# A sandwich of latent attention and a ternary feed-forward layer: another order for the chain of tiles 2 and 3 before the first feed-forward stage, and the signs of four weight pieces on GpSimd

## What is computed

```python
def reference(hidden_states, Wq, bq, Wk, bk, Wv, bv, Wo, bo, latent_keys, W_up, W_gate, W_down):
    def attn(h):                                   # h [2, 2048, 512], 16 heads of 32
        Q, V = h @ Wq.T + bq, h @ Wv.T + bv
        logits = einsum('bhtd,lhd->bhtl', Q, latent) / sqrt(32)      # 64 latents per head
        top, idx = top_k(logits, 4)
        weighted = softmax(top) @ latent[idx]
        return (weighted + V) @ Wo.T + bo
    def ternary(w):
        scale = mean(abs(w)) + 1e-8
        return clip(round(w / scale), -1, 1) * scale
    def ffn(h):                                    # 512 -> 2048 -> 512
        return (silu(h @ ternary(W_up).T) * (h @ ternary(W_gate).T)) @ ternary(W_down).T
    x = x + layernorm(attn(layernorm(x)))
    return x + layernorm(ffn(layernorm(x)))
```

## Time and profile before

| | |
|---|---|
| three executions | 1032.02, 1033.41 (median), 1034.98 us |
| the profiled execution | 1034.87 us, its span 1033.0 us |
| mean granted TensorE clock | 0.982 |
| PE busy | 968.6 us (94%) |
| DVE, ACT, POOL busy | 729.7, 514.2, 535.9 us |

### The profile page before, as it was taken

How to read it: one execution, slowest core, us unless ns; L and a number is a source line. 1 busy time by engine, 2 the same in 40 slices (tenths; PEclk the granted TensorE clock), 3 DMA queues, 4 the chain that set the end, 5 groups by cost and what they waited for, 6 DMA issues and landing times.

```text
span 1033.0 us, 17908 instructions
## 1 busy us (share of the span) xinstructions
PE 968.6 (94%) x5738; PEld 470.2 (46%) x5738; DVE 729.7 (71%) x2665; ACT 514.2 (50%) x801; POOL 535.9 (52%) x452
## 2 busy tenths in 40 slices
PE   3738899999999999999999999999999999999997
PEld 2413444445444554445444454445444454445443
DVE  7998699366993689755993768836895669845433
ACT  5887886445535455245544455345553454423430
POOL 3566256645565446564565446654465546642330
PEclk9869899999999999999999999999999999999999
DMA  9963503442134402234114321253022411212001
GB/s 289 401 110 62 154 1 82 115 90 82 22 42 102 107 16 41 61 81 102 21 21 102 71 72 21 41 118 96 10 41 61 94 40 21 42 41 62 1 1 41
DMA packets 149330, 76.91 MB, mean 74 GB/s; under 512 B 135824, under 2 KB 135824, under 8 KB 148112
## 3 DMA queue, kind: packets, MB, share of 16 engines
q1 hardware_dynamic: 149264, 76.18, 29.7%
HBM read 34.21 MB, written 8.39 MB: 41 GB/s over the span
## 4 chain that ended last, share of the span: by engine, by line
PE 52%; DVE 21%; issue 8%; POOL 8%; ACT 7%; DMA 3%; SPq 0%; DVEq 0%; ACTq 0%; POOLq 0%
PE ug L709 33%; PE ug L728 9%; PE ring L559 6%; DVE Lr L1581 2%; PE ring L687 2%; PE ring L605 2%; POOL halves L1297 2%; DMA X1T<-halves 2%; DVE halves L1535 2%; DVE v L1555 1%; DVE row L1672 1%; DVE x L1692 1%; DVE stx L1695 1%; DVE sty L1675 1%; DVE ugt L1540 1%
## 5 line engine op out<-in xcount | busy, mean ns | idle before, releaser
L709 PE MATMUL ug<-X1T,TU 128*128 128x512 f16 (+1 forms) x1152 | 246.7, 357 | 11.0 <-DMA X1T<-halves 6.7
L1274 POOL TENSOR_TENSOR hT<-ugt,hT 128x512 f16<-128x512 f32 x128 | 167.1, 1305 | 165.6 <-ACT hT L1026 165.6
L709 PE MATMUL ug<-X1T,TG 128*128 128x512 f16 (+1 forms) x1152 | 245.7, 356 | 0.0
L728 PE MATMUL ug<-TD,hT 128*128 128x512 f16 x960 | 210.9, 379 | 0.9 <-ACT TD L905 0.9
L1013 ACT ACTIVATE ugt<-ug,cu 128x512 f32<-128x512 f32 x128 | 88.0, 687 | 207.5 <-PE ug L709 206.6
L709 PEld LDWEIGHTS ug<-X1T,TU 128*128 128x128 f16 x1152 | 110.6, 98 | 122.1 <-issue 9.9
L709 PEld LDWEIGHTS ug<-X1T,TG 128*128 128x128 f16 x1152 | 113.2, 98 | 109.1
L1540 DVE SCALAR_TENSOR_TENSOR ugt<-ugt,ug 128x512 f32<-128x512 f32 x128 | 87.3, 682 | 103.3 <-ACT ugt L1013 102.0
L728 PEld LDWEIGHTS ug<-TD,hT 128*128 128x128 f16 x960 | 93.2, 98 | 115.8 <-issue 3.0
L1581 DVE MATCH_REPLACE8 Lr<-v,Lb 128x68 f32<-128x68 f32 x512 | 102.3, 212 | 0.0
L1545 DVE SCALAR_TENSOR_TENSOR ugt<-ugt,ug 128x512 f32<-128x512 f32 x128 | 87.9, 687 | 4.4
(11 more groups left out here) (217 smaller groups left out, 1498.7 us busy)
## 6 DMA issues: line engine op xcount, KB each, us to landing
out_dram<-Lr SPq DMA_DIRECT2D x32, 256.0 KB, 3.2
x_in<-in_x SPq DMA_DIRECT2D x7, 1024.0 KB, 5.3
x<-in_x SPq DMA_DIRECT2D x28, 256.0 KB, 3.3
PT<-in_Wd SPq DMA_DIRECT2D x8, 512.0 KB, 7.2
hT<-in_Wu SPq DMA_DIRECT2D x4, 512.0 KB, 9.2
hT<-in_Wg SPq DMA_DIRECT2D x4, 512.0 KB, 15.2
x_in<-in_Wd SPq DMA_DIRECT2D x4, 512.0 KB, 4.8
x_in<-in_x SPq DMA_DIRECT2D x4, 256.0 KB, 4.1
```

Source lines behind the costliest of these rows:

```text
L709: last = pe.matmul(ug[:, 2 * (e % 2) + s, cols], w[:, k, e * P:(e + 1) * P], X1T[:, b, k, cols], start=(k == 0 and b == 0), stop=(k == KD ...
L728: last = pe.matmul(down_bank(kind, t), hT[:, a, e, t * P:(t + 1) * P], td[:, e, :], start=(first and e == of[0] and a == 0), stop=(final a ...
L1274: pool.tensor_tensor(hT[:, 1, e, :], ugt[:, 2 + e % 2, :], hT[:, 0, e, :], ALU.subtract).then_inc(h_lo, 1)
```

## The change

It has two parts.

In the first body, DVE does `y_a(2)` before `y_b(1)`, `y_a(3)` before the low half of tile 0, and both `y_b` and all `y_c` of tiles 2 and 3 ahead of every rounding but that of piece 8. ACT does `t2_rows` of tile 2 right behind `q(0)`, that of tile 3 right behind `q(1)`, and the signs of 1 and 9 after both. The rounding of piece 8 goes from POOL to DVE, that of piece 0 stands further ahead on POOL.

In the second body's loop, the signs of pieces 6, 14, 7 and 15 go from ACT to POOL, as two `TENSOR_SCALAR` passes over 1024 elements each (`sign_of`): one in place in float32 (add, max with -1), one that writes the float16 matrix (min with 1). They stand behind `hidden_lo` of `e` = 2, 3, 5 and 6. DVE's roundings of 11, 6 and 14 stand earlier, and ACT has the signs of 10, 5 and 3 one step earlier.

```diff
+        SIGN_POOL = (6, 14, 7, 15)
+        def after_pool(n):
+            return len(ROUND_POOL) + 2 * SIGN_POOL.index(n) + 2
...
+                        if e // 2 in SIGN_POOL:
+                            pe.wait_ge(pool_step, after_pool(NPIECE + e // 2))
...
+                    if kind == "second" and e in (8, 12):
+                        act.wait_ge(pool_step, after_pool(e // 4 + 4))
...
-                SIGN_AT = {0: (2,), 1: (10,), 2: (5, 13), 3: (3, 11), 4: (6,), 5: (14,), 6: (7, 15), 8: (22,), ...
+                SIGN_AT = {0: (2, 10), 1: (5,), 2: (13, 3), 3: (11,), 8: (22,), ...
...
+                def sign_of(n):
+
+                    src = stages[n // NPIECE][n % NPIECE]
+                    pool.wait_ge(rounded, rounded_before(n))
+                    pool.tensor_scalar(src, src, -MAGIC, -1.0, ALU.add, ALU.max).then_inc(pool_step, 1)
+                    pool.wait_ge(pool_step, after_pool(n) - 1)
+                    pool.tensor_scalar(matrix(n), source(n), 1.0, None, ALU.min).then_inc(pool_step, 1)
...
+                    if late and e in (2, 3, 5, 6):
+                        sign_of(SIGN_POOL[(2, 3, 5, 6).index(e)])
...
-                    AFTER = {0: [(round_to, 3)], 1: [(round_to, 11)], 2: [(round_to, 6), (maxes, 0, 0), (maxes, 0, 1)],
-                             3: [(round_to, 14), (slots, 0), (replace, 0, 0)], 4: ...
+                    AFTER = {0: [(round_to, 3), (round_to, 11)], 1: [(round_to, 6), (round_to, 14)], 2: [(maxes, 0, 0), (maxes, 0, 1)],
+                             3: [(slots, 0), (replace, 0, 0)], 4: ...
```

More of the change, by code:

```diff
@@ L273, in build @@
         ASUM_ACT = (0, 1, 16, 17, 18, 19) + tuple(range(4, 14)) + tuple(range(20, 24))
-        TERN_ORDER = (0, 8, 1, 9, 4, 12, 2, 10, 5, 13, 3, 11, 6, 14, 7, 15, 22, 23, 16, 17, 20, 21, 18, 19)
+        TERN_ORDER = (0, 8, 1, 9, 4, 12, 2, 10, 5, 13, 3, 11, 22, 23, 16, 17, 20, 21, 18, 19)
         ROUND_ACT = (18, 19)
-        ROUND_POOL = (0, 8)
+        ROUND_POOL = (0,)
+        SIGN_POOL = (6, 14, 7, 15)
+        ROUND_ORDER = (8, 1, 9, 4, 12, 2, 10, 5, 13, 3, 11, 6, 14, 7, 15, 22, 23, 16, 17, 20, 21)
+        def after_pool(n):
+            return len(ROUND_POOL) + 2 * SIGN_POOL.index(n) + 2
         def rounded_before(n):
-            return sum(q not in ROUND_POOL for q in TERN_ORDER[:TERN_ORDER.index(n) + 1])
+            return ROUND_ORDER.index(n) + 1
         def after_tern(*pieces):
@@ L1101, in body @@
                     q(0)
-                    sign(1)
                     t2_rows(-1, 2)
-                    sign(9)
                     q(1)
                     t2_rows(-1, 3)
+                    sign(1)
+                    sign(9)
+                    q(2)
                     sign(4)
-                    q(2)
                     sign(12)
@@ L1269, in round_to @@
                     pool.wait_ge(tern_scale, w + 1)
-                    pool.tensor_scalar(src, src, iw[:, w:w + 1], MAGIC, ALU.mult, ALU.add).then_inc(pool_rounded, 1)
+                    pool.tensor_scalar(src, src, iw[:, w:w + 1], MAGIC, ALU.mult, ALU.add).then_inc(pool_step, 1)
+                def sign_of(n):
[4 more added lines that the diff above has]
+                    pool.tensor_scalar(matrix(n), source(n), 1.0, None, ALU.min).then_inc(pool_step, 1)
                 def hidden_lo(e):
                     wait(pool, h_hi, j, NE, e + 1)
+                    if kind == "second" and e in (8, 12):
+                        pool.wait_ge(pool_step, after_pool(e // 4 + 12))
                     pool.tensor_tensor(hT[:, 1, e, :], ugt[:, 2 + e % 2, :], hT[:, 0, e, :], ALU.subtract).then_inc(h_lo, 1)
@@ L1776, in body @@
                     y_b(0)
+                    y_a(2)
+                    y_c(0, 0)
+                    tern_total(1)
                     y_b(1)
-                    y_c(0, 0)
+                    y_a(3)
+                    t2_lo(0, 0)
                     y_c(0, 1)
[L1780 to L1783, removed]
                     tern_scale_of(1)
-                    round_to(1)
+                    round_to(8)
                     y_b(2)
                     t2_lo(0, 1)
+                    y_c(0, 2)
+                    y_b(3)
+                    t2_lo(0, 2)
+                    y_c(0, 3)
+                    round_to(1)
+                    t2_lo(0, 3)
                     round_to(9)
-                    y_b(3)
-                    y_c(0, 2)
                     round_to(4)
-                    y_c(0, 3)
-                    t2_lo(0, 2)
                     round_to(12)
-                    t2_lo(0, 3)
                     round_to(2)
```

16 lines of the change are left out of this document (8 added, 8 removed).

## The result

The changed kernel took **1042.72 us** (median of five executions, 1041.86 to 1044.28), against 1033.41 before (five executions, 1032.02 to 1036.05): ratio 1.0089, 95% interval 1.0074 to 1.0105. It is slower by 9.3 us. The forecast was 1032.4, with a range of 1029.2 to 1035.0, so the time lies far outside, on the slow side. The profiled execution took 1042.75 us, its span is 1040.6.

The account below looks back on a forecast made before the run. PE, busy 94% of the span, was taken to bound the kernel, with ACT and then DVE setting the loop's pace. The sum 6.4 - 0.9 - 4.6 + 0.1 = 1.0 us gave 1032.4 us, range 1029.2 to 1035.0.

Parts of the forecast that it names:

- the opening: First body: PE's 4.1 us wait for transposed tiles 2 and 3 goes, its clock stays up, `upgate(2)` starts 6.4 us earlier.
- 3.34 for the transfer: Opening: time from DVE's last operation on tile 3 at 102.4 until PE can go on, at 105.75.
- a pass of two float32 operations over 1024 elements took POOL 1.12 us: Loop, GpSimd's signs: the price of each sign's first pass, taken from a row of the trace.
- 1.3 for the second: Loop, GpSimd's signs: assumed price in us of the float16 pass, making four signs 10.0 us.
- The bound above, 2.14: Loop, GpSimd's signs: upper bound in us for the float16 pass, from a float16 operation on two inputs.
- own signs of being wrong: Wrong if `ffn_scales` stays short, POOL has pauses before 140, or a float16 pass costs far from 1.3 us.
- In itself that delays nobody: Loop: POOL's lump of signs, without pause until about 143.7, delays nobody, as pieces 6 and 14 are needed only by `upgate(12)`.
- The lock: Loop, `hidden(5)` to `hidden(8)`: DVE's operations wait for GpSimd's, 4.8 us less 0.3 idle; `hidden(8)` 0.9 us ahead instead of 5.5.
- rounding of 15 as before: Loop, behind `hidden(5)`: the first of DVE's seven operations open to blocking keeps its time.
- PE's new wait: Loop, near 143: PE waits some 4.5 us for `hidden(8)`, its clock falls, and `upgate(10)` starts at 147.0.
- Rival B: Loop: slower, since the second pass costs 2.14 and DVE's turns lengthen; 1036 to 1037 us, chance 0.11.
- Rival A: Loop: the gain is kept, as POOL isn't full at `ffn_scales` or DVE wins turns; 1029 to 1030 us, chance 0.27.

Follow-up runs that it names:

- e1: The changed kernel with the signs of 6, 14, 7 and 15 back on ACT, new opening and tables kept: 1028.73 us, 0.9955 of the kernel before.
- e5: The change's new opening alone, with the loop tables of the kernel before and all signs on ACT: 1029.12 us, 0.9958 of before.
- e3: The changed kernel with GpSimd's first pass a multiply-add and its second a multiply alone, pieces not clipped: 1035.23 us, 1.0013 of before.
- e8: The changed kernel with both GpSimd passes as multiply-adds, pieces not cut to signs: 1032.61 us, 0.9992 of before.
- e7: The changed kernel with GpSimd's eight passes one behind each low half of tiles 2 to 9: 1042.11 us, 1.0080 of before.
- e13: The changed kernel with the four signs made by no engine, PE reading columns of tiles 4 to 7 again: 1031.15 us, 0.9970 of before.
- e14: As e13, with one wait more that holds GpSimd's shift until the rounding of piece 15 is done: 1028.91 us, 0.9953 of before.
- e11: The changed kernel with one multiply-add a piece on GpSimd, straight to the matrix, not cut to signs: 1032.21 us, 0.9982 of before.

## Why the prediction was wrong

**What bounds the kernel, and the opening: right, with one duration too small.** Sign of 8 ended at 94.8 (forecast 95.1), tile 3's low half at 102.53 (102.4), `tanh(4)` came at 124.37 (123.9). PE's wait fell to 0.89 us and its clock stayed up at 107 to 108. The term "3.34 for the transfer" was too small: from DVE's last low half to PE it takes 4.87 us (102.53 to 107.40), of which the last transposes are 4.58 in the chain, and why they took longer in the new order isn't shown. So PE goes on at 107.40, not 105.75, and `upgate(2)` is 4.85 us earlier, not 6.4. By their ratios the whole gains 4.6 us in e1 and 4.3 in e5.

**The step that failed: "a pass of two float32 operations over 1024 elements took POOL 1.12 us", and 1.3 for the second.** The row was a multiply-add; the change's pass is an add and a max. It takes 3.64, and the second 2.77: four signs are 26 us, not 10.0. The price was taken from a row of the same instruction and shape with other operations in it. The bound above, 2.14, was too low as well, and for the first pass no bound was given, since the row was taken for its own. e3 and e8 show each half of this: with the first pass at 1.04 the time is 1035.2, with both at 1.04 it is 1032.6. So of the 14.0 us that the signs cost, 10.1 are the price of the passes. Two of the prediction's own signs of being wrong came with it: a float16 pass far from 1.3 us, and short `ffn_scales`.

The Trainium skill (GPSIMD Engine Reference, 3.1 Elementwise), by which up to two operations cost 1.03 cycles an element (an estimate of 0.88 us for 1024), agrees with the 1.04 to 1.06 of multiply-add, add-multiply and copy. For the other forms the measured 2.78 and 3.63 or more decide against it.

**"In itself that delays nobody" falls with the price.** It was reasoned from when the pieces are needed. The queue behind the passes was counted for the lock only, while the low halves in it release DVE's next buffer. At 10 us it would have held: in e8 DVE waits for no low half. At 26 us it cost 8.9 us of waits on DVE, and PE's two long waits with the low clock behind them. e7 shows that the low halves are not the only ones in the queue: spread out, the same passes delay the shift, at the same cost.

**The lock (DVE's operations that wait out one of GpSimd's): a right sum with a wrong cause.** The prediction put 4.6 us on DVE between `hidden(5)` and `hidden(8)` and left `hidden(8)` 0.9 us ahead. With its own prices (e8) it was 3.93, and `hidden(8)` started at 145.44 (forecast 145.55). But "rounding of 15 as before" was wrong: 2.40 us in place of 0.94. And e13 shows 2.87 (14.57 against 11.70) of the 3.93 with no pass at all, e14 that one meeting with the shift starts it. The prediction named the passes; they add only the rest. In the changed kernel itself the slow passes held DVE less than forecast: `ffn_scales` at 147.34 took 0.15 us with the second pass of piece 7 under way since 145.83. The holds that it did have are the slots' difference (1.16 us at 141.07 for 0.16), `select(0)` (2.07 for 1.21) and the rounding of 22 (1.56 at 145.85 for 0.75): 2.7 us where 4.8 were forecast.

**PE's new wait, and luck in e8's time.** With the prediction's prices (e8) PE waits 1.67 us for DVE's scale (`sw`) at 141.31 and 1.28 for `hidden(8)`, not 4.5 in one piece, and the granted clock is 1.00 in each microsecond from 140 to 149, so nothing is lost to a low clock. `upgate(10)` starts at 146.98, as forecast (147.0), but by errors that cancel: `upgate(2)` was 4.43 us ahead in place of 6.4, and `hidden(5)` 4.96 ahead, so the lead grew where the sum took 0.9 off. That e8's 1032.6 lies so near to 1032.4 is in part luck.

**Rival B** had the direction and, for a second pass of 2.14, 1036 to 1037; e3, whose first pass is cheap and whose second is 2.78, takes 1035.2. Half of its mechanism is there, a second pass that makes POOL's queue longer. But it reckoned with longer turns of DVE and not with waits for the low halves (1.31 and 4.46 us ahead of `hidden(8)`, which started at 149.65, 3.2 later than before). Its chance was put at 0.11 on the strength of a row that didn't show the operation. Rival A's 1029 to 1030 was reached by no run with passes on GpSimd; e14, with no passes and no meeting, took 1028.9. **And nothing that was tried let the second half of the change win**: with the four signs taken from every engine the best time was 1028.9, with them on ACT 1028.7.

## What to carry to other kernels

A GpSimd row prices only its own operations: same instruction, shape and types aren't enough, and a pass without a row of its own needs a wide upper bound. Before work goes to an engine with room, list what stands behind it in that engine's queue and who waits for that, and try first what the kernel gains if the work is done by nobody. Where DVE and GpSimd are both near a stretch's pace, look at which of two meeting operations starts first: one wait that changes it was worth some 2 us here.

## What the runs showed of the hardware that was not expected

- `TENSOR_SCALAR` on GpSimd over 128x1024: 1.04 to 1.06 us with an add and a multiply, 2.8 with one operation alone (but 3.8 for max), 3.6 to 4.0 with two others. A neutral `* 1.0` ahead of an add is cheaper by 1.7 us than the add alone (1.04 against 2.78).
- A slow pass didn't hold DVE's operation on 128x1 that began in its middle (147.34, 0.15 us), nor, in e3, the rounding at 131.40 (0.75 us) inside the pass from 130.32 to 133.09. Low halves did hold (142.46, 1.12 us beside 142.24 in e11), and a multiply-add did (143.53, 0.97 us beside 143.46 in e3). The Trainium skill (GPSIMD Engine Reference, 8. Key points) has one rule for both, two SBUF inputs on Vector; what of GpSimd's own instruction decides was not tried. At a slow pass's start DVE was held (142.16: 2.07 us for 1.21), so the moment at which DVE begins may count as well as the form; the runs don't part the two.
- Who starts first pays little: the rounding at 131.13, before the shift at 131.47, took 0.95 us (e1; 0.75 in e14, where the shift stands behind it), and the rounding at 131.58, behind the shift at 131.32, took 2.22 (e11).
